# Second expert layer: mixed blocks' weights copied on ScalarE from the resident ones, first two row gathers issued in the route

## What is computed

```python
shared = silu(xt @ Wg_s) * (xt @ Wu_s) @ Wd_s
logits = xt @ W_router + routing_bias
probs = jax.nn.sigmoid(logits)
scores, idx = jax.lax.top_k(probs, TOPK)
scores = scores / jnp.sum(scores, axis=-1, keepdims=True)
wts = jnp.sum(jax.nn.one_hot(idx, ER, dtype=xt.dtype) * scores[..., None], axis=1)
g = jnp.einsum('th,ehi->tei', xt, Wg_r)
u = jnp.einsum('th,ehi->tei', xt, Wu_r)
hmid = silu(g) * u
combined = jnp.einsum('tei,eih,te->th', hmid, Wd_r, wts)
return (shared + combined).reshape(B, S, H)
```

## Time and profile before

| | us |
|---|---|
| median of 3 runs (lowest, highest) | 1716.93 (1716.62, 1720.66) |
| the profiled execution's own time | 1715.14 |
| its span, first to last instruction | 1713.2 |
| stage `kept_blocks`, from TensorE's first instruction in it to its last | 966.0 to 1089.3 |

### The profile page before, as it was taken

One profiled execution on the slowest core, in us unless ns is written; L12 is line 12 of the kernel. 1 busy time (PEld: TensorE's weight loads), 2 busy tenths in 40 slices (PEclk: granted clock), 3 DMA queues, 4 the chain that ended last, 5 costly groups with the idle time before them and its releaser, 6 DMA issues. The chain is left out here.

```text
span 1713.2 us, 33545 instructions
## 1 busy us (share of the span) xinstructions
PE 1485.6 (87%) x11942; PEld 1126.6 (66%) x11975; DVE 945.3 (55%) x2428; ACT 498.5 (29%) x1047; POOL 485.1 (28%) x585
## 2 busy tenths in 40 slices
PE   4887899999979986899978899677888797899995
PEld 3664799999968853455545455345666575699995
DVE  4556244444448968666637433489887556422221
ACT  2331111111147745465532122223331333011010
POOL 0102344444410002111112243342111110466663
PEclk9999999999988997899999999888899999999998
DMA  4209677777720005433305467210000004688885
GB/s 139 51 2 308 218 210 232 210 230 213 222 59 1 2 2 165 130 89 112 86 22 197 143 212 260 67 45 25 1 1 1 2 2 156 197 242 234 233 241 147
DMA packets 147445, 218.73 MB, mean 128 GB/s; under 512 B 21377, under 2 KB 96897, under 8 KB 147137
## 3 DMA queue, kind: packets, MB, share of 16 engines
q1 hardware_dynamic: 121792, 183.57, 32.9%
q0 software_dynamic: 20640, 29.16, 8.2%
q10 hardware_dynamic: 4896, 4.46, 0.8%
HBM read 184.59 MB, written 34.64 MB: 128 GB/s over the span
## 5 line engine op out<-in xcount | busy, mean ns | idle before, releaser
L1575 DVE TENSOR_REDUCE l1a_nm<-l1a_sc 128x1 f32<-128x512 f32 (+3 forms) x256 | 107.2, 483 | 53.6 <-PE l1a_sc L1711 53.6
L2446 ACT ACTIVATE e0b_sg<-e0b_gp 128x640 f32<-128x640 f32 x78 | 33.5, 481 | 266.1 <-PE e0b_gp L2386 266.1
L2359 POOL DMA_INDIRECT y_sum<-e0b_yb,e_token x39 | 63.1, 1619 | 140.5 <-DVE e0b_yb L2473 137.5
L2359 POOL DMA_INDIRECT y_sum<-e3b_yb,e_token x39 | 62.7, 1607 | 61.5 <-DVE e3b_yb L2473 58.6
L2446 ACT ACTIVATE e3b_sg<-e3b_gp 128x512 f32<-128x512 f32 x39 | 23.3, 597 | 189.5 <-PE e3b_gp L2386 189.5
L1709 PEld LDWEIGHTS l1a_sc<-l_stack_k,l_stack_q 128*128 128x128 bf16 x256 | 25.3, 99 | 60.9 <-issue 26.9
L1711 PE MATMUL l1a_sc<-causal_h,ident_h 128*128 128x128 bf16 x256 | 47.0, 223 | 19.9 <-PEq L1353 15.5
L2465 DVE TENSOR_TENSOR e0b_hT<-e0b_up,e0b_sg 128x640 f32<-128x640 f32 x39 | 32.2, 825 | 57.8 <-PE e0b_up L2386 57.8
L2753 POOL TENSOR_TENSOR f_hq<-f_q,f_q 128x704 f32<-128x704 f32 x16 | 22.9, 1432 | 135.7 <-DVE f_q L2740 135.7
L1470 POOL TENSOR_TENSOR xn<-xn 128x512 f32<-128x512 f32 x8 | 10.1, 1266 | 178.2 <-DVE xn L1438 178.2
L2386 PEld LDWEIGHTS e0b_gp<-e0b_xT,e0k_wgu 128*128 128x128 f32 x480 | 58.4, 197 | 1.9 <-DVE e0b_xT L2458 0.9
(11 more groups left out here) (637 smaller groups left out, 4015.1 us busy)
## 6 DMA issues: line engine op xcount, KB each, us to landing
e3k_wgu<-in_L_ffn_W SPq DMA_DIRECT2D x40, 512.0 KB
e3b_wgu<-in_L_ffn_W SPq DMA_DIRECT2D x38, 512.0 KB
e0k_wgu<-in_L_ffn_gate_proj SPq DMA_DIRECT2D x20, 704.0 KB
e0k_wgu<-in_L_ffn_up_proj SPq DMA_DIRECT2D x20, 704.0 KB
e0b_wgu<-in_L_ffn_gate_proj SPq DMA_DIRECT2D x19, 704.0 KB, 4.2
e0b_wgu<-in_L_ffn_up_proj SPq DMA_DIRECT2D x19, 704.0 KB, 5.5
x_rows<-xn SPq DMA_DIRECT2D x3, 2048.0 KB, 8.4
l_parts<-l1p_split SPq DMA_DIRECT2D x16, 384.0 KB, 3.1
```

The source lines that it names most:

```text
L1575: nc.vector.tensor_reduce(nm[:, g % 2, q, i:i + 1], sc[q], AX_X, ALU.max, negate=True).then_inc(max_done, 1)
L2359: pool.indirect_dma_start(y_sum, bass.IndirectOffsetOnAxis(ap=token[:, n:n + 1], axis=0), yb[n % 2][:], None, compute_op=ALU.add).then_inc ...
L2446: last = nc.scalar.activation(sg[rows, chunks, :], gp[rows, chunks, :], ACT.Silu)
```

## The change

- `kept_blocks` no longer loads weights from HBM. ScalarE copies each mixed block's weights from the resident ones: 8 copies of 128x512 (gate and up, 2 for each of the four owners) and 8 of 128x256 (down) for a set. It reads the four owners into its own registers. Set 0 begins before the first block (2 copies, behind a wait for `kept`) and goes on with up to 6 copies a block; the later sets begin in the iteration of the mixed block before and get 4 copies a block, behind silu(n) and copy_hidden(n-1).
- TensorE waits in a mixed block for the 8 copies of gate and up, and ahead of its down product for all 16.
- The gathers of blocks 0 and 1 are issued by GpSimd in `route`, behind a new wait for `token` (semaphore `routed`). The later gathers take their index straight from `token`; the small copy and the tiny addition are gone.
- SP issues the stores of the blocks to `y_slots`, each as soon as copy_out(n) is done.
- The 14 filling matmuls at the start are gone.

```diff
@@ experts
+                    xb = [s2.enter_context(nc.sbuf_tensor(f"{tag}_xb{j}", [P, D], F32)) for j in range(2)]
...
-                            route(tag, lp, E, wt, slot, owner, token, bias, x, outer, beside_route, lay=lay)
-                    kept_blocks(tag, kept_gu, kept_d, (kept, 16 * len(fills[0] + fills[1])), F, lay, E, owner, token,
-                                (w_gate, w_up, w_down))
+                            route(tag, lp, E, wt, slot, owner, token, bias, x, outer, beside_route, lay=lay, first_rows=xb)
+                    kept_blocks(tag, kept_gu, kept_d, (kept, 16 * len(fills[0] + fills[1])), F, lay, E, owner, token, xb)
@@ route, GpSimd
+                    if first_rows is not None:
+                        pool.wait_ge(routed, 1)
+                        pool.wait_ge(sent, 16)
+                        for n in range(2):
+                            pool.indirect_dma_start(first_rows[n][:], None, x_rows, bass.IndirectOffsetOnAxis(ap=token[:, n:n + 1], axis=0))\
+                                .then_inc(rows_in[n], 16)
@@ route, VectorE
-                        nc.vector.tensor_copy(token[:], token_f[:])
+                        nc.vector.tensor_copy(token[:], token_f[:]).then_inc(routed, 1)
@@ kept_blocks, SP
-                    def load_mixed(i):
...
-                    load_mixed(0)
-                    load_mixed(1)
-                    for n in mixed_at[:-2]:
-                        sp.wait_ge(y_made, n + 1)
-                        load_mixed(mixed_at.index(n) + 2)
+                    for n in range(NB):
+                        sp.wait_ge(y_copied, n + 1)
+                        sp.dma_start(y_slots.rearrange("(n p) d -> n p d", p=P)[order[n]], yb[n % 2][:]).then_inc(rows_out[n % 2], 16)
@@ kept_blocks, GpSimd
-                    for n in range(NB):
-                        if n >= 2:
-                            pool.wait_ge(x_turned, n - 1)
-                        nc.gpsimd.tensor_copy(index[n % 2][:], token[:, order[n]:order[n] + 1]).then_inc(index_ready, 1)
-                        pool.wait_ge(index_ready, n + 1)
-                        nc.gpsimd.tensor_tensor(spare[:], const("place"), const("place"), ALU.add)
-                        pool.indirect_dma_start(xb[n % 2][:], None, x_rows, bass.IndirectOffsetOnAxis(ap=index[n % 2][:], axis=0))\
+                    for n in range(2, NB):
+                        pool.wait_ge(x_turned, n - 1)
+                        pool.indirect_dma_start(xb[n % 2][:], None, x_rows,
+                                                bass.IndirectOffsetOnAxis(ap=token[:, order[n]:order[n] + 1], axis=0))\
                             .then_inc(rows_in[n % 2], 16)
@@ kept_blocks, TensorE
-                            pe.wait_ge(mixed_in[i % 2], MIXED_IN * (i // 2 + 1))
+                            pe.wait_ge(mixed_ready, OF_SET * mixed_at.index(n) + OF_GU)
...
+                        if is_mixed(n):
+                            pe.wait_ge(mixed_ready, OF_SET * (mixed_at.index(n) + 1))
...
-                    stay_busy(gu[0][:], 14)
@@ kept_blocks, ScalarE
-                    def store(n):
...
+                    def set_of(i):
+
+                        n = mixed_at[i]
+                        es = [act.value_load(owner[0:1, at:at + 1], min_val=0, max_val=experts_n - 1) for at in lay.owner_at(order[n])]
+                        if i >= 2:
+                            act.wait_ge(y_made, mixed_at[i - 2] + 1)
+                        for u, e in enumerate(es):
+                            for k in range(KC):
+                                yield mixed_gu[i % 2][:, u, k, :], wgu[:, bass.ds(e, 1), k, :].rearrange("p a f -> p (a f)")
+                        for u, e in enumerate(es):
+                            for f in range(FC):
+                                yield mixed_d[i % 2][:, u, f, :], wd[:, bass.ds(e, 1), f, :].rearrange("p a d -> p (a d)")
+
+                    def copy_some(pieces, count):
+                        for to, source in itertools.islice(pieces, count):
+                            nc.scalar.copy(to, source).then_inc(mixed_ready, 1)
 
                     act.preload_act_table(ACT.Silu)
+                    act.wait_ge(*kept)
+                    pieces = set_of(0)
+                    copy_some(pieces, 2)
                     for n in range(NB):
...
-                        if n >= 3:
-                            store(n - 3)
+                        following = [i for i in range(len(mixed_at)) if mixed_at[i] > n]
+                        if n in mixed_at and following:
+                            pieces = set_of(following[0])
+                        if following:
+                            copy_some(pieces, -(-OF_SET // (mixed_at[following[0]] - 1 - (mixed_at[following[0] - 1] if following[0] else 0))))
```

More of the change, by code:

```diff
@@ L8 @@
+import itertools
 from contextlib import ExitStack
@@ L1951, in add, with route @@
                 nc.vector.tensor_tensor(self.into[:, tiles, :], self.yp[g][:], self.into[:, tiles, :], ALU.add).then_inc(self.added, 1)
-    def route(tag, lp, E, wt, slot, owner, token, bias, x, outer, beside=None, plan=None, lay=None):
+    def route(tag, lp, E, wt, slot, owner, token, bias, x, outer, beside=None, plan=None, lay=None, first_rows=None):
         NB = ROUTED if lay is None else lay.blocks
@@ L1993, in route @@
                 pair_i, tile_i, tile_f = tmp("pair_i", [P, ROUTED], U32), tmp("tile_i", [P, ROUTED], U32), tmp("tile_f", [P, ROUTED])
-                tabled, left_cleared, routed = sem("tabled"), sem("left"), sem("routed")
+                tabled, left_cleared = sem("tabled"), sem("left")
             if beside is None:
@@ L1999, in route @@
                 summed = sem("summed")
+            routed = sem("routed")
             sent, hot, token_made = sem("sent"), sem("hot"), sem("token")
@@ L2493, in _, with kept_blocks @@
                     weigh_out(NB - 1, 0, NB // 2)
-    def kept_blocks(tag, wgu, wd, kept, F, lay, experts_n, owner, token, weights):
+    def kept_blocks(tag, wgu, wd, kept, F, lay, experts_n, owner, token, xb):
         FC, NB, PER = F // P, lay.blocks, lay.per
@@ L2505, in kept_blocks @@
             ps = lambda n, s: st.enter_context(nc.psum_tensor(f"{tag}b_{n}", s, F32))
-            xb, xT, h, hT, yb = ([tmp(f"{n}{j}", m) for j in range(2)] for n, m in (
-                ("xb", [P, D]), ("xT", [P, KC, P]), ("h", [P, F]), ("hT", [P, FC, P]), ("yb", [P, D])))
+            xT, h, hT, yb = ([tmp(f"{n}{j}", m) for j in range(2)] for n, m in (
+                ("xT", [P, KC, P]), ("h", [P, F]), ("hT", [P, FC, P]), ("yb", [P, D])))
             sg = [tmp(f"sg{j}", [P, F]) for j in range(2)]
@@ L2510, in kept_blocks @@
             xp, hp = ps("xp", [P, 2 * KC, P]), ps("hp", [P, 2 * FC, P])
-            index = [st.enter_context(nc.sbuf_tensor(f"{tag}b_index{j}", [P, 1], U32)) for j in range(2)]
-            spare = tmp("spare", [P, 1])
+            before = list(blocks_before)
+            blocks_before[0] += (NB + 1) // 2
+            blocks_before[1] += NB // 2
             mixed_gu = [tmp("mixed_gu", [P, PER, KC, 2 * F]),
@@ L2515, in kept_blocks @@
             mixed_d = [tmp("mixed_d", [P, PER, FC, D]), xnT[:, 0, :].rearrange("p (u f d) -> p u f d", u=PER, f=FC)]
[L2516 to L2521, removed]
+            mixed_ready, OF_GU, OF_SET = sem("mixed"), PER * KC, PER * (KC + FC)
+            x_turned, x_copied, gu_made, sg_done, h_done, h_turned, h_copied, y_made, y_copied = (
+                sem(n) for n in ("xt", "xc", "gu", "sg", "h", "ht", "hc", "ymade", "yc"))
             with nc.Block() as block:
@@ L2575, in gate_up @@
                         if is_mixed(n):
-                            i = mixed_at.index(n)
-                            pe.wait_ge(mixed_in[i % 2], MIXED_IN * (i // 2 + 1))
+                            pe.wait_ge(mixed_ready, OF_SET * mixed_at.index(n) + OF_GU)
                         for k in range(KC):
@@ L2648, in _ @@
                             copy_hidden(n - 1)
-                        if n >= 3:
-                            store(n - 3)
+                        following = [i for i in range(len(mixed_at)) if mixed_at[i] > n]
[3 more added lines that the diff above has]
+                            copy_some(pieces, -(-OF_SET // (mixed_at[following[0]] - 1 - (mixed_at[following[0] - 1] if following[0] else 0))))
                     copy_hidden(NB - 1)
-                    for n in range(NB - 3, NB):
-                        store(n)
                 @block.vector
```

2 lines of the change are left out of this document (removed).

## The result

The changed kernel takes 1707.22 us in the median of 8 runs (1703.92 to 1710.29), beside 1719.46 (1713.71 to 1725.09, 8 runs) of the kernel before: 0.9929, with a 95% interval from 0.9910 to 0.9948. It is faster, by 12.2 us in the medians; the interval stands for a gain of 8.9 to 15.5. A second timing later gave 1705.17 (6 runs) beside 1715.30 (11 runs), 0.9936 [0.9920, 0.9953]. The profiled execution of the changed kernel took 1703.92 us, with a span of 1702.0.

A forecast was written before the change was run, and what follows sets the result against it. The prediction took the blocks to be bound by TensorE with small holes from late gathers, the start not. Start 6.8, clock 0, gathers 5.7 and ScalarE 0 made 12.5 us: 1716.93 to 1704.4, range 1701.0 to 1710.5.

The forecast's parts named there:

- The start: Ahead of block 0: with early gathers TensorE turns rows at 966.02 instead of 972.81, gaining 6.8 us.
- The clock: At the first gate_up: TensorE's granted clock drops again as before, gain 0, from -0.5 to 1.4 us.
- Rival B: At the start: the clock holds thanks to shorter idle, 1.4 us more gained, 1703.0 us; chance 0.27.
- The gathers: In the blocks: without the weight loads, gathered rows land in time and TensorE's holes go, gaining 5.7 us.
- rival D: In the blocks: gathers stay late by GpSimd's and HBM's own time, 5.7 us not gained, 1710.1 us; chance 0.08.
- The half microsecond of GpSimd: Ahead of each gather: dropping index copy and addition saves some 0.5 us, about 3 in all if landings stayed.
- ScalarE, 0 us: Behind mixed blocks: ScalarE's reads and copies make silu late, but just inside the slack, costing 0 us.
- the estimate of 2.5 to 6 us: On ScalarE: cost over five sets if each owner read took the skill page's floor of about 600 ns.
- Rival C: Behind mixed blocks: ScalarE becomes the bound through slow reads or copies, 3 us, 1707.4, up to 6; chance 0.16.
- Rival E: On ScalarE: copies with a register address cost much more, eating all gain from 0.93 us each, 1727.9 us; chance 0.05.
- Rival F: At the start: another wait takes its place, and only half of the gathers' 5.7 us is gained, 1714.0; chance 0.06.
- A: The forecast itself for the whole kernel: 12.5 us gained, 1704.4 us; chance 0.38.

The follow-up runs named there:

- x1: The kernel before with the first two gathers issued in the route and no filling matmuls; loads, index copies and ScalarE's stores kept; 1712.71 us.
- x5: The changed kernel with 3 filling matmuls between the first turning of rows and the first gate_up; 1707.12 us.
- x6: The changed kernel with 3 filling matmuls between first turning and first gate_up, and 4 behind the route's last product; 1706.58 us.
- x7: The changed kernel with the 14 filling matmuls of the kernel before put back ahead of the first turning; 1707.25 us.
- x3: The kernel before without the weight loads of sets 2 to 5, later mixed blocks using earlier sets' weights; 1717.13 us.
- x2: x1 with the gathers also taking their index straight from `token`, without the small copy and addition; loads kept; 1712.80 us.
- x9: The changed kernel with ScalarE reading one of each set's four owners a second time; 1707.97 us.
- x10: The changed kernel with ScalarE reading two of each set's four owners a second time; 1708.65 us.
- x4: The changed kernel with ScalarE reading all four of each set's owners a second time; 1719.44 us.
- x12: The kernel of x6, timed in 6 runs; 1703.13 us, 0.9931 of the kernel before.

## Why the prediction was right, point by point

**The start, 6.8 us.** Right: 8.53 to 1.75 in the changed kernel, and the same in x1, where it stands alone. The rows of block 0 were there, block 2's gather, issued at 964.78, held nobody up, and GpSimd had nothing else to do while it waited for `token`.

**The clock, 0.** Right in this trace and in the eight others that have 1.75 us of idle right ahead of the first turning (first gate_up 3.20 to 3.38 us). Rival B fell. x5 and x6 bracket the cause: an idle stretch of 1.75 us ahead of one turning was enough for the drop even with the 0.71 behind it filled, and with 0.99 and the 0.71 filled there was none. The row that spoke for B, 2.26 us without a drop, was followed at once by 11 filling matmuls, and so was x7's 1.75 by 14, without a drop either: the length of the gap alone doesn't decide. x5, too, had no idle left behind its 1.75, and its clock fell, so what tells it from x7 stays open, with one trace of each. B priced the drop at 1.4 us; x6 and x7 measure 1.6.

**The gathers, 5.7 us.** The stage gained 6.03. The mechanism was the one named: x3 shows that the loads alone carry 5.21, and rival D, that the gathers are late by themselves, falls with it. The landings came to a median of 2.8, where "near 2.7" was forecast, and the DMA engines to 77 GB/s for "near 80". The half microsecond of GpSimd was put at "about 3" if the landings stayed; it was 0.4, and x2 has 2.16. The sum over the timeline of late beats was nearer than the waits' column, which has 4.2.

**ScalarE, 0 us.** Right, with the terms nearly as forecast. Reads: 2.0 forecast, 1.86 to 1.88 measured in four sets and 2.15 in one. Copies: 0.52 to 0.61 apiece, measured 4 in 2.18, so one every 0.52. One term was too small: the sum has 0.45 us from silu to the start of the reads' stretch, where it is 0.93 (979.64 to 980.57), because `copy_hidden`'s own time belongs to it. Reads of 1.86 instead of 2.0 and copies at the low end of their range made up for it: 0.93 + 1.86 + 2.08 = 4.87, inside the 4.5 to 4.9, which is luck in part. The silu was to be 1.5 to 1.9 late, and is 1.72, then "1.3 to 2.0", and is 1.31 (987.12, where 985.60 + 0.21 = 985.81 would be its place). The slack was taken as 2.0; it is 1.72 + 0.34 = 2.06, set by `copy_rows`, the instruction that was named. TensorE's own wait, for `turn_hidden`, comes at 1.72 + 0.48 = 2.20 (985.34 to 985.82), close behind, and is the one that the view of waits shows once it is overrun. So "little cover" was the right word: over the five sets, one more read in each costs 1.8 us (x9), two cost 4.3 (x10).

The Trainium skill (DMA: Bandwidth & Descriptors, Latency and other measured facts) gives a floor of about 600 ns for a tensor load. The trace disagrees for a read of an owner from SBUF: 277 ns, and 150 of register work behind it. The measurement decides, and the estimate of 2.5 to 6 us that hung on that figure didn't come true. Where reads are added, though, each lengthens the gap by 0.45 to 0.8 (x9, x10, x4), mostly more than the rows' 0.45. The first four may hide a part of theirs behind silu and `copy_hidden`; that is argued, not shown.

**Rival C's price was mis-sized.** The case didn't come (no TensorE wait for `hidden` in the changed kernel), but it priced an overrun at its length. x4 shows that an overrun of some 2 us can cost 1.5 to 1.6 more, because the clock fell behind two of its five (3.87 lost in the beat behind block 4, of which the sum of gap and room explains 4.45 - 1.87 - 0.34 = 2.24). Had the reads been as slow as in C's worst case (all four at 797 ns, 2.0 us a set), the price could have been well above the 6 us of the range: x4, with 1.9 to 2.2 of overrun a set, lost 13.2.

**Rival E**, which needed copies at an address in a register to cost 0.93 us or more, didn't come: they cost 0.52 to 0.55. **Rival F**, another wait in the start's place and half of the gathers' gain, didn't come either.

**The sum.** 12.5 us forecast, 6.78 + 6.03 = 12.8 in the traces, 12.2 and 10.1 between the medians. The totals alone would not have decided between A, B and F: gains of 12.5, 13.9 and 9.7 all lie in the interval of 8.9 to 15.5. The stage and its start in the traces do. The two profiled executions differ by 11.2 only (1715.14 and 1703.92), though the stage and its start gave 12.8. Of before it takes 623.9 us from the stage's last matmul to the end of the span (1713.2 - 1089.3), of after 628.5 (1702.0 - 1073.55), while what lies ahead of the stage went the other way by 2.9. Both are the size of the spread between executions that share all these instructions (625.7 to 633.0 and 960.9 to 967.5), so nothing points to the change. x1 to x3, which share before's instructions behind the stage, take 630.3 to 632.3 there, so it is before's 623.9 that was short. That the change has no effect at all on later stages was only argued and isn't shown to better than some microseconds.

The forecast of 1704.4 is 2.8 below the median of 1707.22, and 2.5 of that is the median of before itself, which was 1716.93 when the forecast was made and 1719.46 beside the result.

## What to carry to other kernels

The small late transfers here were cured by taking away the large ones beside them, and only helped by issuing them earlier; once the large ones were gone, the earlier issue was worth nothing, so two such gains mustn't be added untested. When work is moved to an engine with room, compare its lateness with the first instruction that slips: add a few tenths of a microsecond to it on purpose and see from where the stage grows. Price an overrun on TensorE's path at more than its length, since the clock can fall behind it.

## What the hardware showed that was not expected

- In x4 TensorE, in a stretch in which it is otherwise nearly always busy, waited once in each of five sets. Behind the waits of 2.00 and 1.62 us the clock fell to 0.50, which made the beats 1.6 and 1.5 longer than the overrun explains; behind those of 1.64, 1.70 and 1.78 it stayed up. What decides between them stays open.
- At the start an idle stretch of 1.75 us right ahead of the first turning was followed by the drop in all nine traces that have it, whether or not the next 0.7 us were filled (one of them, x5, has it filled). With 4 matmuls of 1.03 us in all in its first part, which left 0.99 in one piece, and the 0.7 us filled too, the clock stayed (x6, x12). It also stayed with 14 filling matmuls between the 1.75 us and the turning (x7, one trace). No rule that covers all of these is shown.
- A gather of 128 rows lands in 2.8 us (2.6 to 3.6) when only the other gathers and the stores of results run beside it, and in 4.3 (2.7 to 6.7) beside loads of 256 KB.
- ScalarE's 128x512 copy from SBUF to SBUF shows 619 ns each, but four in a row take 2.18 us: one every 0.52.
